# A two-layer hybrid transformer on one core: shorter steps in the chain between the layers, division on GpSimd, a smaller entry, a reordered recurrent stage

## The reference

```
x = x + window_attention(norm(x))      # 16 heads of 8, window 32, token 0 global
x = x + ternary_linear(norm(x))
x = x + recurrent(norm(x))             # two directions: gates, linear scan, gelu, linear
x = x + ternary_linear(norm(x))
x = x + attention_a(norm(x))           # full attention, 16 heads; out = num / (den + 1e-8); bias bo
x = x + experts(norm(x))               # top 1 of 8, capacity by order of tokens, shared We, gate = probability
x = x + attention_b(norm(x))           # full attention, 16 heads
x = x + experts(norm(x))
```

## Time and profile before

| | us |
|---|---|
| runs | 1139.51, 1146.8, 1138.41; median 1139.51 |
| profiled execution | 1144.26, its span 1142.4, mean granted TensorE clock 0.908 of full speed |
| busy in the span | TensorE 1001.0, VectorE 833.4, ScalarE 752.0, GpSimd 132.4 |
| ends of the stretches, from the span's start | window attention 212, norms with the ternary and recurrent blocks 323, entry 358.6, full attention 1088, last run 1142.4 |

### The profile page before, as it was taken

How to read it: one execution, slowest core, us unless ns; L and a number is a source line. 1 busy time by engine, 2 the same in 40 slices (tenths; PEclk the granted TensorE clock), 3 DMA queues, 4 the chain that set the end, 5 groups by cost and what they waited for, 6 DMA issues and landing times.

```text
span 1142.4 us, 32326 instructions
## 1 busy us (share of the span) xinstructions
PE 1001.0 (88%) x13347; PEld 463.9 (41%) x13347; DVE 833.4 (73%) x1023; ACT 752.0 (66%) x1497; POOL 132.4 (12%) x416
## 2 busy tenths in 40 slices
PE   6799999782768999999899899999989999999964
PEld 2455455330333344444344344444434444344433
DVE  5446653536546999999779689978879997799412
ACT  3504446265431799998767689877779977699911
POOL 8100110000000000000102120010221001010000
PEclk8789999886877999999989899999999998899975
DMA  3753442100035132301000034200005410010000
GB/s 102 227 169 75 102 98 62 29 1 1 1 104 174 39 74 52 80 18 28 12 11 15 19 107 116 60 12 13 12 22 140 107 36 11 11 45 19 19 15 19
DMA packets 60386, 64.47 MB, mean 56 GB/s; under 512 B 17424, under 2 KB 39184, under 8 KB 60112
## 3 DMA queue, kind: packets, MB, share of 16 engines
q1 hardware_dynamic: 60240, 62.40, 20.6%
HBM read 27.06 MB, written 35.32 MB: 55 GB/s over the span
## 4 chain that ended last, share of the span: by engine, by line
DVE 48%; PE 38%; issue 5%; ACT 4%; DMA 3%; SPq 1%; POOL 0%; POOLq 0%; ACTq 0%; DVEq 0%
DVE nmf L1607 40%; PE wide L658 24%; PE bank L658 13%; DVE xcsq L1378 1%; DVE xp L1378 1%; ACT xcsq L1139 1%; DMA x<-xT 1%; ACT big L1139 1%; ACT L1139 1%; DVE xcsq L1387 1%; DVE big L1765 1%; ACT scr L1139 1%; SPq L433 1%; DMA KQs<-mw_dram 1%; DVE x L1378 1%
## 5 line engine op out<-in xcount | busy, mean ns | idle before, releaser
L1607 DVE TENSOR_REDUCE nmf<-wide 128x1 f32<-128x1024 f32 x512 | 591.0, 1221 | 50.5 <-PE wide L658 50.2
L1139 ACT ACTIVATE big<-wide 128x512 f32<-128x512 f32 x684 | 392.1, 602 | 92.9 <-PE wide L658 82.0
L658 PE MATMUL wide<-big,KQs 48*128 48x512 bf16 (+1 forms) x1376 | 358.8, 350 | 5.5 <-DVE nmf L1607 4.2
L658 PE MATMUL bank<-big,V 128*9 128x128 f32 x8192 | 328.8, 279 | 11.5
L658 PE MATMUL wide<-KQs,big 50*128 50x512 bf16 (+1 forms) x1036 | 273.2, 329 | 6.1 <-ACT big L1139 6.1
L658 PEld LDWEIGHTS bank<-big,V 128*9 128x9 f32 x8192 | 178.4, 91 | 239.4 <-ACT big L1139 194.2
L1139 ACT ACTIVATE big<-bank 128x512 f32<-128x512 f32 (+1 forms) x468 | 232.5, 515 | 45.2 <-PE bank L658 39.5
L658 PE MATMUL bank<-KQs,big 50*128 50x512 bf16 x340 | 133.0, 391 | 3.9 <-ACT big L1139 3.9
L1139 ACT ACTIVATE scr<-wide 128x380 f32<-128x380 f32 (+3 forms) x128 | 61.4, 487 | 84.2 <-PE wide L658 73.0
L658 PEld LDWEIGHTS wide<-KQs,big 50*128 50x128 bf16 x1036 | 70.3, 95 | 113.9 <-ACT big L1139 58.5
L1552 DVE TENSOR_REDUCE nmw<-wide 95x4 f32<-95x512 f32 (+1 forms) x96 | 60.7, 637 | 53.2 <-PE wide L658 52.3
(11 more groups left out here) (214 smaller groups left out, 813.1 us busy)
## 6 DMA issues: line engine op xcount, KB each, us to landing
o_dram<-big SPq DMA_DIRECT2D x128, 64.0 KB
big<-kf_dram SPq DMA_DIRECT2D x32, 200.0 KB
kf_dram<-scr SPq DMA_DIRECT2D x24, 256.0 KB, 3.3
qf_dram<-scr SPq DMA_DIRECT2D x24, 256.0 KB, 3.9
KQs<-qf_dram SPq DMA_DIRECT2D x32, 192.0 KB
ow_dram<-scr SPq DMA_DIRECT2D x32, 142.5 KB
big<-kw_dram SPq DMA_DIRECT2D x16, 275.0 KB
kw_dram<-scr SPq DMA_DIRECT2D x12, 352.0 KB, 5.6
```

The source lines that it names most:

```text
L658: return nc.tensor.matmul(o, l, r, start=start, stop=stop, **kw)
L1139: return nc.scalar.activation(o, i, f, **kw)
L1607: nc.vector.tensor_reduce(nmf[:, i % 4, c:c + 1], wide[:, k:k + 2, :].rearrange("p g c -> p (g c)"), AX.X, ALU.max, negate=True).then_inc( ...
```

## The change

- **Recurrent stage.** The forward input products move into the norm before the stage and the backward ones between the gates; GpSimd does x + xn, the squares, and the multiplies of batch 1; ScalarE takes roots only, in the order `ORDER` (batch 0 first); a scan starts when its batch's pieces are done; output products stand among fillers; the bias goes into the gelu and the evacuation by ScalarE is gone; one VectorE operation instead of two makes the new x.
- **Entry.** Only batch 0 is projected. SyncE stores and loads k, ScalarE's queue q, the first quarter of the heads ahead; the means are spread after the projections; batch 1's projections become steps at ticks 12 to 23.
- **Chain.** Five runs over chunks (0, 1), (2, 3), (0, 1), (2), (3), starting at slots 35, 67, 99, 115 and 128. `sel` is left to the last run; the others store their reciprocals to DRAM, load them back with every sum repeated over its head's eight rows, and GpSimd multiplies (`div`). `mean` becomes `centre`: one product with I - 1/128, copied out by ScalarE (in the last run squared by it too). Most steps are taken chunk by chunk at two neighbouring ticks. The largest logit is found before the exponential, so `prob` has fewer operations. The last run has fillers (`FILL`), and VectorE does its addition.

The core of the diff (the renamed semaphores and the widths that follow are left out):

```diff
-RUNS = 4
+RUN_LAYER = (1, 1, 2, 2, 2)
+RUN_CHUNKS = ((0, 1), (2, 3), (0, 1), (2,), (3,))
+RUNS = len(RUN_CHUNKS)
...
-        TICK = {"sel": 0, "wo": 3, "mean1": 6, "square1": 8, "var1": 12, "std1": 14, "rstd1": 17, "norm1": 19, "logits": 23,
...
-        START = tuple(4 * (ALL_SLOTS * (r + 1) // RUNS + (3 if r < 3 else 0)) for r in range(RUNS))
+        TICK = {"den": (0,), "sel": (0,), "div": (11,), "wo": (14, 15), "centre1": (17, 18), "square1": (19,), "var1": (23, 24),
+                "std1": (26,), "rstd1": (27,), "norm1": (29, 30), "logits": (32,), "onehot": (34,), "exp": (34,),
+                "we": (35, 36), "total": (37,), "count": (38,), "gate": (42, 43), "add": (43,),
...
+        START = (4 * 35, 4 * 67, 4 * 99, 4 * 115, 4 * ALL_SLOTS)
+        PSTART = (12, START[0] + 63, START[1] + 63)
+        FILL = {"sel": 26, "wo": 3, "centre1": 3, "var1": 6, "norm1": 4, "logits": 3, "gate": 8}
...
+        def first_batch(eng, k):
+            eng.wait_ge(fp_third, 2 * k + 2)
+            for j in range(6):
+                store_heads(eng, k, 0, j, 0, H // 4, part_first[k])
+            for j in range(6):
+                store_heads(eng, k, 0, j, H // 4, H, part_out[k])
+            eng.wait_ge(part_first[k], 96)
+            load_heads(eng, k, 0)
+            eng.wait_ge(part_out[k], 96)
+            load_heads(eng, k, 1)
...
+                def sums_spread(r):
+                    sp.wait_ge(d_out, 16 * summed(r + 1))
+                    for c in RUN_CHUNKS[r]:
+                        sp.dma_start(xch(xc, c), d_dram[4 * (RUN_LAYER[r] - 1) + c, :, :, :].rearrange("h c q -> h (c q)")
+                                     .unsqueeze(1).broadcast_to((H, D, 512))).then_inc(d_in, 16)
...
+                    for r in range(LAST):
+                        if i == START[r] // 4 + SPREAD:
+                            sums_out(r)
+                        if i == START[r] // 4 + SPREAD + 1:
+                            sums_spread(r)
...
+                if name == "div":
+                    for j, c in enumerate(RUN_CHUNKS[r]):
+                        pool.wait_ge(o_in[c], 16 * RUN_LAYER[r])
+                        pool.wait_ge(d_in, 16 * summed(r + 1))
+                        pool.tensor_tensor(xch(aT, c), xch(aT, c), xch(xc, c), ALU.mult).then_inc(c_div, 1)
...
+                    if name in ("centre1", "centre2"):
...
+                        mm(score_entry(s_index[r, name, j]), cent[:, :], xch(x, c)).then_inc(sc_ready, 1)
...
+                    if name in ("centre1", "centre2"):
...
+                        fn(xch(xc, c), bk(4 + e % 3), ACT.Copy).then_inc(sc_exp, 1)
...
+                for n in range(2 * NC):
+                    pool.wait_ge(r_decay, n + 1)
+                    a = rb[:, 1, 512 * n:512 * n + 512]
+                    pool.tensor_tensor(rc[:, 512 * n:512 * n + 512], a, a, ALU.mult).then_inc(r_square, 1)
...
+                keep_busy(24, bk(7))
+                outs(0, 0)
+                keep_busy(5, bk(7))
+                outs(1, 0)
+                keep_busy(4, bk(7))
+                outs(0, 1)
+                outs(1, 1)
```

More of the change, by code:

```diff
@@ L1708, in full_attentions @@
                         turn(UNITS + i // 2 - 1, UNITS + i - 1)
[L1709 to L1714 removed]
+                    for r, name, j in steps_at(tick):
+                        chain(r, name, j)
+                    for p, name in projections_at(tick):
+                        project(p, name)
             def add_projection():
```

681 lines of the change are left out of this document (369 added, 312 removed).

## The result

The changed kernel takes 1148.09 us, median of 20 runs (1142.16 to 1155.87), against 1140.78 for the kernel before on the same chip, 20 runs (1133.06 to 1147.46). The ratio is 1.0077, 95% interval 1.0058 to 1.0096: slower, though by less than the 1% that was set as the bound. The forecast was 1090, with 1072 to 1110 as its range. The profiled execution of the changed kernel took 1148.46, its span 1146.7, at a mean granted clock of 0.919; against the profiled span before, 1142.4, that is +4.3.

The account below looks back on a forecast made before the run. In attention VectorE and TensorE were taken as nearly equal bounds, both left waiting by chain passes. Terms -20 - 13 + 8 - 12 + 15 - 27 = -49 took 1139.5 to 1090 us, range 1072 to 1110.

Parts of the forecast that it names:

- recurrent stage: Stage before attention: squares on GpSimd, earlier scans and full-clock output products save 20 us.
- entry to the first maximum: Entry to layer 1: projecting only batch 0 and loading the first heads early saves 13 us, between 9 and 17.
- batch 1's projections in attention: Batch 1's projection steps, moved into attention, cost 8 us, taken from the same steps for layer 2.
- chain passes 1 to 3: Passes inside attention: less VectorE work and halved steps, less new waits for GpSimd, save 12 us.
- fourth pass: Chunk 2 leaves the tail for its own 512-column pass in attention, costing 15 us, between 13 and 20.
- tail: Last chain pass to the end: 512 columns at full clock save 27 us, 14 if the clock stays at half.
- the new wait: VectorE's turns wait for GpSimd's split, about 2.5 us behind the division and 1.8 behind the addition.
- if halving gave nothing +5: Bound for passes 1 to 3 in attention: with no gain from halving they cost 5 us.
- rival B: Clock stays low in tail and recurrent stage, 13 + 5 us lost, 1108 us; chance 8%.
- The bound at -16.5: Recurrent stage saves only 16.5 us if GpSimd's four multiplies take twice 1.25 us beside VectorE.
- A (GpSimd's queue): Division in attention's passes comes later than reckoned, 5 us more in each of four, 1110 us; chance 12%.
- D: Slower than before: the broadcast read of repeated sums delays each of four divisions, about 1160 us; chance 5%.

Follow-up runs that it names:

- e7: Changed kernel without the filler products of the last pass; 1156.69 us (one run).
- e6: Changed kernel with GpSimd's division four ticks later and its addition one later, behind the second split, projection and centring later too; 1123.58 us, ratio 0.9877 to the kernel before.
- e9: Changed kernel with early loads, 74 entry fillers, division and addition behind the second split, and all eight multiplications before the scans on VectorE; 1100.92 us, ratio 0.9635.
- e10: e9 with output projection, variances, normalisation and gate as whole steps of 1024 columns again; 1098.83 us, ratio 0.9645 to the kernel before.
- e12: e9 with the centring as a product with 1/128 that VectorE subtracts from x again, without ScalarE's copies; 1099.6 us.
- e13: e9 with 58 entry fillers instead of 74; 1113.17 us, ratio 0.9786 to the kernel before.
- e11: e9 with the division by selection-matrix products on TensorE and VectorE multiplications again, without broadcast transfers; 1110.14 us, ratio 0.9749 to the kernel before.
- e2: Changed kernel with the first four heads' keys and queries loaded before the other twelve heads are stored; 1141.78 us, ratio 1.0044 to the kernel before.
- e5: Changed kernel with the first four heads loaded before the others are stored, and 78 entry fillers instead of 18; 1127.35 us, ratio 0.9899 to the kernel before.
- e8: Changed kernel with all eight multiplications ahead of the scans on VectorE again, squares staying on GpSimd; 1148.61 us (one run).
- e1: Changed kernel with 96 instead of 18 fillers before the attention's first maximum; 1148.93 us, ratio 1.0013 to the kernel before.

## Why the prediction was wrong, step by step

| step | forecast | measured in the span |
|---|---|---|
| recurrent stage | -20 | -16.9 |
| entry to the first maximum | -13 | -2.5 |
| preload at half clock | not counted | +14.7 |
| batch 1's projections in attention | +8 | +7.8 |
| chain passes 1 to 3 | -12 | +13.9 |
| fourth pass | +15 | +13.8 |
| tail | -27 | -25.7 |
| undisturbed stretches | 0 | -0.8 |
| sum | -49 | +4.3 |

The +14.7 are 6.8 to the first turn and 7.9 of the 15.8 to the sixth; the other 7.8 are the two intervals with the projections, 12.07 and 14.01 instead of 9.14. Three steps were right within 1.5 us: projections, fourth pass, tail. Two of them owe it in part to luck. The fourth pass was worked out from the third, taken as 26 us; the third then cost 31.9 (86.7 less 54.8 undisturbed), which by the same sum gives 18, and it was 13.8. In the tail the -27 were 13 for the clock and 14 for the rest; e7 shows 6.6 and 19. Those that failed:

**"Chain passes 1 to 3, -12": 26 us off, in two parts.** First, the new wait. The place was right, a turn behind the division and one behind the addition; the size was 2.5 us between 1.3 and 4, and 1.8. Measured: 4.5 and 1.44. Even the forecast's own terms (landed 3.3 to 4.5 after the evacuation, 2.9 of GpSimd's work, 3.7 until the turn) make 2.5 to 3.7, so 2.5 was their lower end. In the new trace slot 36's evacuation has ended when its output is issued at 552.83; GpSimd starts at 558.30, 5.5 later. The issues begin 0.7 after it, behind the output's own, and take 1.49 instead of 1.2, and the landing of the second follows them in full. But the size of the waits is the smaller error: the sum has 14.5 us for them over three passes (-12.5 against -27), 17.9 were measured, and taking them away gave back 24.7 in e6's trace. Second, and larger, the gain beside it. Without waits I counted 11 us for a full pass, 27 for three; e6, e9, e10, e12 and e13 show 8 to 16, and e11 that the division makes up what can be seen of it. The 0.5 for each halved step and 1.7 for each halved variance, and the subtractions taken from VectorE, can't be told from nothing. The likely reason, which the sums bear out but no row shows step by step: a halved step finds its product ready, and a later maximum waits instead, for the same TensorE work, which halving doesn't lessen. Over the three passes VectorE stands idle for 74.7 us in e9 and 74.1 in e10 (time less busy time in the sums above), and for 72.1 before. The text itself gave this case as "if halving gave nothing +5"; it should have been the base. (A slip beside it: 11 less the 5.1 of waits is 5.9 for a full pass, not 5.5.)

**"Entry, -13": 25 us off, in two parts.** The first maximum was expected at 324 (344 less 20) and came at 339.2, 15.2 us later. Of these, 3.1 are the recurrent stage's. Another 2.9 lie ahead of the stores: they were to start 26.5 after the last x (329.4), for batch 1 was no longer projected, but start 29.4 after it, as before (29.3); why nothing was gained there stays open. The other 9.2 are the way from the first store to the first maximum, 23.8 instead of 14.6: I moved the transfers' bytes at 262 GB/s, but while they are issued they move at 160, and the early quarter's loads stood behind all the stores of their queue. e2 and the kernels after it show the second to be worth 6 to 7. The Trainium skill (Trainium Kernel Development and Optimization, Key Constraints) says that several queues share the DMA engines and save issue time alone. The trace agrees: the rate did not rise. Nor was ScalarE's queue quick to issue, at 1.22 us each. And the idle time of TensorE got a price of "1 to 2 us" less where it cost 14.7, because I took the clock as a matter of the tail and the recurrent stage (rival B) and not of the entry, where the change takes the fillers away from the place that they protect. e5 and e9 to e12 show that the early loads and fillers that end at the first maximum repair both.

**"Recurrent stage, -20": 3 us off.** The bound at -16.5 was nearer: GpSimd's four multiplications took 2.2 us each in the mean (1.7 to 3.2) beside VectorE instead of 1.25, its squares 1.42 instead of 1.02, VectorE's own two 3.37 instead of 1.4, and its three scans behind them 8.62, where three alone take 6.9 (2.29 each in e8). The Trainium skill (GPSIMD Engine Reference, Key points) says that the two contend when VectorE reads two SBUF inputs. These rows agree, and they show that VectorE loses by it too, which the sum had left out. e8 confirms it from the other side.

Of the rivals, A (GpSimd's queue) had the mechanism of the new wait, but with 1110 as its result, because its 20 us stood against a sum that was too good; D, the one on the slow side, blamed the repeated read, which landed in 3.4 to 3.7 us as the row without repetition does. The observation that was to prove me wrong, "if VectorE waits over 5 us at such a turn, or if the first passes cost 50 again", came true in its second half: 142.9 us less the 91.4 of ten undisturbed intervals are 51.5.

## What to carry to other kernels

On an in-order engine place every chain step behind the short operation that others wait for, not in front of it: the same division four ticks later (and the addition one later) was worth 23 us here. Cutting a step in two is no gain by itself: the halved steps waited less, and the passes were no shorter within the 8 us of scatter. Count it only if the producer's work shrinks too. When a change shortens or moves work ahead of a stretch that runs at full clock, recount the fillers: they have to last until the operand is there, and too many cost 0.22 us each, as long as one took in e1, while a gap cost 14.

## What the runs showed of the hardware that was not expected

- The granted clock stayed at 0.50 through 17.66 us in which TensorE was busy throughout (e13_gap), with pairs of 512-column bfloat16 products of 48 and of 128 rows in turn; the same pairs at 1.00 kept 1.00 (e9_combined). The first had a gap of 3.14 us ahead of them, the second none; behind a gap of 2.72 us (e1_fill) the pairs began at 1.00 and fell to 0.50 after 2 us.
- A transfer of 64 or 192 KB took ScalarE's queue 1.22 us to issue and SyncE's 0.83 when both issued twelve at once. With the loads put between (e2, e5), the first six took 3.83 us on SyncE and 4.6 on ScalarE.
- Two multiplications from SBUF on VectorE beside GpSimd's took 3.37 us instead of 1.29, and a scan up to 3.3 instead of 2.29: both engines lose, more than the split of the work gains.
